# Graph convolution edge stage: how many pairs of edge tiles are in flight between four engines

## What is computed

```
h = silu(edge_scalars @ fc_w1 / sqrt(8))       # 8 scalars per edge, 64 hidden
w = h @ fc_w2                                  # 256 weights per edge: w_a, w_b, w_c, w_d
xg = y[edge_src]                               # 256 features gathered per edge
mid = w * xg, times the 4 numbers edge_attr    # products per edge
agg = segment_sum(mid, edge_dst)               # added up by destination node
```

## Time and profile before

| | |
|---|---|
| median of three runs | 5709.57 us |
| the profiled execution, its own time | 5680.69 us |
| its span | 5678.8 us |
| busy over the span: PE, weight loads, DVE, ACT, POOL | 72%, 53%, 54%, 44%, 53% |
| edge stage, from its first `collect` to the last `add` | about 227 to 2001 us |

### The profile page before, as it was taken

How to read it: one execution, slowest core, us unless ns; L and a number is a source line. 1 busy time by engine, 2 the same in 40 slices (tenths; PEclk the granted TensorE clock), 3 DMA queues, 4 the chain that set the end, 5 groups by cost and what they waited for, 6 DMA issues and landing times. The chain is left out here.

```text
span 5678.8 us, 102477 instructions
## 1 busy us (share of the span) xinstructions
PE 4061.7 (72%) x21623; PEld 3009.8 (53%) x21624; DVE 3040.8 (54%) x7561; ACT 2499.3 (44%) x7826; POOL 3007.1 (53%) x3072
## 2 busy tenths in 40 slices
PE   2789998988998885477777777754267777777770
PEld 1577777777777773344455444532144545544450
DVE  5766666666665655345554444542245444454457
ACT  2566666766666622233333333321133333333342
POOL 2255554555555502566666666512456666666645
PEclk7899999999999997666665666665566666566665
DMA  3322222222222223344443344311334333444424
GB/s 116 105 70 70 72 72 67 73 70 70 71 70 69 71 93 100 98 117 114 115 116 105 113 116 116 98 31 44 99 104 114 111 109 114 116 114 116 115 68 138
DMA packets 253117, 533.46 MB, mean 94 GB/s; under 512 B 65502, under 2 KB 139673, under 8 KB 252916
## 3 DMA queue, kind: packets, MB, share of 16 engines
q0 software_dynamic: 136768, 380.16, 24.2%
q1 hardware_dynamic: 109128, 145.00, 8.1%
q10 hardware_dynamic: 7020, 6.40, 0.3%
HBM read 489.95 MB, written 41.38 MB: 94 GB/s over the span
## 5 line engine op out<-in xcount | busy, mean ns | idle before, releaser
L1118 POOL DMA_INDIRECT arena<-h_rows,idx x1856 | 1904.0, 1026 | 1244.6 <-issue 498.6
L1282 PE MATMUL ps<-arena,z 128*128 128x264 f32 x3712 | 1657.4, 597 | 413.4 <-DVE arena L1391 273.0
L1282 PEld LDWEIGHTS ps<-arena,z 128*128 128x128 f32 x3712 | 973.8, 288 | 739.5 <-issue 469.1
L634 POOL DMA_INDIRECT arena<-y_rows,idx x928 | 878.0, 946 | 841.9 <-DVE arena L819 573.9
L709 ACT ACTIVATE arena<-arena 128x128 f32<-128x128 f32 x3712 | 1133.0, 388 | 348.7 <-DVE arena L803 258.4
L1399 DVE TENSOR_TENSOR z<-ps,z 128x264 f32 x928 | 400.7, 432 | 1134.8 <-PE ps L1282 630.1
L765 PEld LDWEIGHTS ps<-arena 128*128 128x128 f32 x5568 | 808.4, 200 | 64.5 <-issue 8.2
L765 PE MATMUL ps<-arena 128*128 128x128 f32 x5568 | 810.4, 283 | 6.5 <-issue 6.3
L1186 ACT ACTIVATE z<-z 128x256 f32<-128x256 f32 x928 | 380.5, 410 | 949.3 <-PE ps L1282 609.8
L762 PE MATMUL ps<-arena 128*128 128x256 f32 x1856 | 630.9, 423 | 183.3 <-ACT arena L709 127.8
L1178 ACT ACTIVATE z<-iota,dst_x 128x128 f32<-128x128 f32 x1856 | 642.9, 394 | 94.9 <-ACT z L1186 4.0
(11 more groups left out here) (231 smaller groups left out, 3079.8 us busy)
## 6 DMA issues: line engine op xcount, KB each, us to landing
z<-lo_rows SPq DMA_DIRECT2D x116, 512.0 KB
arena<-h_rows,idx POOLq DMA_INDIRECT x1856
arena<-y_rows,idx POOLq DMA_INDIRECT x928
z<-seg_rows SPq DMA_DIRECT2D x232, 64.0 KB
h_rows<-arena SPq DMA_DIRECT2D x98, 132.0 KB, 1.7
arena<-h_rows SPq DMA_DIRECT2D x98, 132.0 KB, 2.1
res_rows<-z SPq DMA_DIRECT2D x98, 128.0 KB, 1.7
arena<-res_rows SPq DMA_DIRECT2D x98, 128.0 KB, 2.1
```

Of the source, the lines that this page charges most:

```text
L634: pool.indirect_dma_start(out=s.ring[:, r, 0:width], out_offset=None, in_=table, in_offset=bass.IndirectOffsetOnAxis(ap=s.idx[:, u, n:n + ...
L1118: pool.indirect_dma_start(out=ring[:, u * SCORED + n, :], out_offset=None, in_=h_rows, in_offset=bass.IndirectOffsetOnAxis(ap=s.idx[:, u, ...
L1282: last = t.matmul(ps[:, bank[q % 4], 0:ROW], sel[:, q % SELS, k, :], ring[:, u * SCORED + 2 * q + k, :], start=(k == 0), stop=(k == 1))
```

## The change

Everything between the engines gets more buffers, and each engine works further ahead in its list:

- `msg`, `sel` and `eq` have four buffers (pair mod 4). `eq` and `e8` become buffers of their own outside the arena, and the others are laid out anew in it.
- The ring has 16 slots, one per slot of a group. The gather of slot n of group g waits until the products of the same place in group g-1 are done, for each pair of slots.
- The second layer of a pair writes one bank: the 512 columns of bank 2 + (pair mod 4). For this `w2` is 512 wide, `fc_w2` stands in rows 0 to 63 of its left half and in rows 64 to 127 of its right half, and the rest is zero. Both matmuls take all 128 rows of `h2`.
- `select` is one comparison of 256 columns in place of two of 128, with both operands broadcast.
- Order for pair n: PE does `first(n+4)` (every other time), `second(n+2)`, `collect(n)`; ACT does `weights(n+2)`, then `silu(n+4)`; DVE does `messages(n+1)`, `select(n+3)`, `add(n-1)`.
- New waits: `weights` waits for `agg_ok` of four pairs before, `messages` too, `select` waits for `sel_ok` of four pairs before, and `second` waits for `msg_ok` of four pairs before. Before, the count of `agg_ok` that `select` waited for stood for the first and the third.

The diff, cut to its core:

```diff
-RING = 8
+RING = GROUP
...
-        s.w2 = sb("w2", [P, FEAT])
+        s.w2 = sb("w2", [P, 2 * FEAT])
...
-            if n % 2 == 0 and not (isinstance(g, int) and g == 0 and n < RING):
-                pool_wait(pool, s, msg_ok, g * 8 + n // 2 - RING // 2 + 1)
+            if n % 2 == 0 and not (isinstance(g, int) and g == 0):
+                pool_wait(pool, s, msg_ok, (g - 1) * 8 + n // 2 + 1)
...
-                sp.dma_start(s.w2[h * 64:(h + 1) * 64, 0:FEAT], a["fc_w2"]).then_inc(wt, 16)
+                sp.dma_start(s.w2[h * 64:(h + 1) * 64, h * FEAT:(h + 1) * FEAT], a["fc_w2"]).then_inc(wt, 16)
...
+            def weights(g, u, n):
+                pair = g * IN + n
                 act.wait_ge(eq_ok, pair + 1)
+                if not early(pair, 4):
+                    act.wait_ge(agg_ok, pair - 3)
...
             def group(g, u, final=False):
+                for n in range(IN):
+                    if not (final and n + 2 >= IN):
+                        weights(*ahead(g, u, n + 2))
+                    if n % 2 == 0 and not (final and n + 4 >= IN):
+                        silu(*ahead(g, u, n + 4))
+                    if n == 0 and not final:
+                        stage(g + 1, 1 - u)
...
                 for k in range(2):
-                    rows = slice(64 * k, 64 * k + 64)
-                    last = nc.tensor.matmul(ps[:, 2 + 2 * b + k, 0:FEAT], h2[rows, q % 2, b, :], s.w2[rows, 0:FEAT], start=True, stop=True)
+                    last = nc.tensor.matmul(ps[:, 2 + n % 4, k * FEAT:(k + 1) * FEAT], h2[:, n // 2 % 2, n % 2, :], s.w2[:, k * FEAT:(k + 1) * FEAT],
+                                            start=True, stop=True)
...
             def group(g, u, final=False):
+                for n in range(IN):
+                    if n % 2 == 0 and not (final and n + 4 >= IN):
+                        first(*ahead(g, u, n + 4))
+                    if not (final and n + 2 >= IN):
+                        second(*ahead(g, u, n + 2))
+                    collect(g, u, n)
...
-                if not (isinstance(g, int) and g == 0 and q == 0):
-                    dve.wait_ge(agg_ok, pair - 1)
-                for k in range(2):
-                    last = v.tensor_scalar(eq[:, b, k, :], s.iota[:, :], s.dst_x[:, bass.ds(pair * 2 + k, 1)], None, ALU.is_equal)
-                last.then_inc(eq_ok, 1)
+                if not early(pair, 4):
+                    dve.wait_ge(sel_ok, pair - 3)
+                v.tensor_tensor(eq[:, n % 4, :, :], s.iota[:, :].unsqueeze(1).broadcast_to([P, 2, P]),
+                                s.dst_x[:, bass.ds(pair * 2, 2)].unsqueeze(2).broadcast_to([P, 2, P]), ALU.is_equal).then_inc(eq_ok, 1)
...
             def group(g, u, final=False):
+                for n in range(IN):
+                    if not (final and n + 1 >= IN):
+                        messages(*ahead(g, u, n + 1))
+                    if not (final and n + 3 >= IN):
+                        select(*ahead(g, u, n + 3))
+                    if n:
+                        add(g, u, n - 1)
+                    elif not (isinstance(g, int) and g == 0):
+                        add(g - 1, 1 - u, IN - 1)
```

More of the change, by code:

```diff
@@ L652, in conv_edges, with ahead, early @@
     eq_ok = s.sem("eq_ok")
-    got = s.swdge("ring", RING, [SLOTS // RING * 16] * RING)
+    got = s.swdge("ring", RING, [GROUPS * 16] * RING)
     got8 = s.swdge("got8_", 2, [0, 0])
-    yg = s.ring[:, :, 0:FEAT]
-    e8, h2 = s.e8, s.h2
+    e8, h2, eq, msg, sel = s.e8, s.h2, s.eq, s.msg, s.sel
     i8 = s.i8[:, :].unsqueeze(2)
-    msg = s.work[:, 0:2048].rearrange("p (b k f) -> p b k f", b=2, k=2)
-    sel = s.work[:, 2048:4096].rearrange("p (b k c n) -> p b k c n", b=2, k=2, c=4)
-    eq = s.eq
     w8 = s.w8[:, :].rearrange("p (q m) -> p q m", q=8)
     ps = s.ps
+    IN = GROUP // 2
     tail = (GROUPS - 1) % 2
+    def ahead(g, u, n):
+        return (g, u, n) if n < IN else (g + 1, 1 - u, n - IN)
+    def early(pair, n):
+        return isinstance(pair, int) and pair < n
     with nc.Block() as block:
@@ L708, in weights @@
                     for c in range(4):
-                        last = nc.scalar.activation(sel[:, b, k, c, :], eq[:, b, k, :], ACT.Copy, scale=s.edge_x[:, c, slot])
+                        last = nc.scalar.activation(sel[:, n % 4, k, c, :], eq[:, n % 4, k, :], ACT.Copy, scale=s.edge_x[:, c, slot])
                 last.then_inc(sel_ok, 1)
             def group(g, u, final=False):
-                for q in range(4):
-                    if q < 3:
-                        silu(g, q + 1)
-                    elif not final:
-                        silu(g + 1, 0)
-                    for b in range(2):
-                        weights(g, q, b)
-                    if q == 1 and not final:
+                for n in range(IN):
[4 more added lines that the diff above has]
+                    if n == 0 and not final:
                         stage(g + 1, 1 - u)
             stage(0, 0)
-            silu(0, 0)
+            silu(0, 0, 0)
+            silu(0, 0, 2)
+            for n in range(2):
+                weights(0, 0, n)
             run_tiles(act, GROUPS - 1, 2, group)
@@ L729, in _, with first @@
             pe.wait_ge(wt, 16 * (GROUP + 2))
-            def first(g, u, q):
+            def first(g, u, n):
+                q = n // 2
+                k = g * (IN // 2) + q
                 if q == 0:
                     pe.wait_ge(got8[u][0], (g - u) * 8 + 16)
-                if not (isinstance(g, int) and g == 0 and q < 2):
-                    pe.wait_ge(h_ok, g * 4 + q - 1)
+                if not early(k, 2):
+                    pe.wait_ge(h_ok, k - 1)
                 for b in range(2):
-                    last = nc.tensor.matmul(ps[:, q % 2, b * P:(b + 1) * P], w8[:, 2 * q + b, :], e8[:, u, :], start=True, stop=True)
+                    last = nc.tensor.matmul(ps[:, q % 2, b * P:(b + 1) * P], w8[:, n + b, :], e8[:, u, :], start=True, stop=True)
@@ L739, in first, with second @@
                 last.then_inc(pre_ok, 1)
[L741 to L746 removed]
+            def second(g, u, n):
+                pair = g * IN + n
+                pe.wait_ge(h_ok, g * (IN // 2) + n // 2 + 1)
+                if not early(pair, 4):
+                    pe.wait_ge(msg_ok, pair - 3)
@@ L754, in collect @@
                 pe.wait_ge(msg_ok, pair + 1)
                 pe.wait_ge(sel_ok, pair + 1)
-                if not (isinstance(g, int) and g == 0 and q == 0):
+                if not early(pair, 2):
                     pe.wait_ge(z_ok, pair - 1)
-                o = ps[:, 6 + b, :]
+                o = ps[:, 6 + n % 2, :]
                 for k in range(2):
-                    m = msg[:, b, k, :]
+                    m = msg[:, n % 4, k, :]
                     o4, m4 = (x[:, 256:512].rearrange("p (q f) -> p q f", q=4) for x in (o, m))
-                    nc.tensor.matmul(o[:, 0:256], sel[:, b, k, 0, :], m[:, 0:256], start=(k == 0), stop=False, skip_group_check=True)
+                    nc.tensor.matmul(o[:, 0:256], sel[:, n % 4, k, 0, :], m[:, 0:256], start=(k == 0), stop=False, skip_group_check=True)
@@ L763, in collect @@
                     for c in range(3):
-                        last = nc.tensor.matmul(o4[:, c:4:3 - c, :], sel[:, b, k, 1 + c, :], m4[:, 0:c + 2:c + 1, :],
+                        last = nc.tensor.matmul(o4[:, c:4:3 - c, :], sel[:, n % 4, k, 1 + c, :], m4[:, 0:c + 2:c + 1, :],
                                                 start=False, stop=(k == 1 and c == 2), skip_group_check=True)
@@ L769, in group @@
             def group(g, u, final=False):
[L770 to L784 removed]
+                for n in range(IN):
[4 more added lines that the diff above has]
+                    collect(g, u, n)
             first(0, 0, 0)
+            first(0, 0, 2)
+            second(0, 0, 0)
+            second(0, 0, 1)
             run_tiles(pe, GROUPS - 1, 2, group)
             group(GROUPS - 1, tail, True)
[L788 removed]
         @block.vector
```

119 lines of the change are left out of this document (47 added, 72 removed).

## The result

After the change the kernel takes 5813.8 us (median of four runs, 5810.8 to 5826.8), before it 5712.6 (four runs, 5692.4 to 5727.1): ratio 1.0193, with an interval of 1.0162 to 1.0223. It is **101 us slower**, not 158 faster. The profiled execution took 5826.8 us, 13 above its median.

A forecast was written before the change was run, and what follows sets the result against it. PE was taken to bound the edge stage. Of 264 us lost there, 92 stay and a slower pace costs 14, so 158 us are won: median 5709.6 to 5552 us, range 5460 to 5690.

The forecast's parts named there:

- Second layer: PE's second layer on all 128 rows: 0.03 us more per pair, +14 us, pace 3.285 us; at most +107 us.
- The price of 204 us: PE's second layer: by the skill alone, undoing half-height packing costs 0.44 us per pair, +204 us; not the value taken.
- The waits: PE's halts in the edge stage: slack grows from 0.8 to 3.15 us; of 264 us lost, 92 stay and 172 go.
- DVE: DVE's single comparison of 256 columns takes 0.43 us against 0.48 for two; 1.0 us to spare, nothing on the path.
- ACT: ACT's copies and silu take 2.9 us, every other pair without silu: costs nothing, 0.4 us to spare, the next bound.
- POOL and the ring: POOL's gathers, 2.66 us a pair, issued up to eight pairs ahead in place of four: priced at nothing.
- Fill and drain: Start and end of the stage: DVE's zeroing comes first in its list before and after, so nothing changes.
- the idle time before L770: Sign of success: PE's idle time before the first matmul of `collect` falls from 183 us to under 70.
- the clock: Sign of success: PE's granted clock in the stage rises from 0.95 to 0.98 or more.
- the sign of being wrong: One stated sign of failure: PE's idle time in the changed kernel is as long as before.
- The slower rival: Gathers bunch on POOL and hold back PE's counts: 4.05 us a pair, 105 us more, 5815 us; chance 0.10.
- Its condition: A count of PE is held back whenever POOL issues, and arrives 1.32 us after its last gather.

The follow-up runs named there:

- experiments 3 and 6: Kernel before with only the full-height second layer: 5816.7 us, ratio 1.002; kernel before without its row gathers: 5486.8 us, ratio 0.937.
- experiment 9: Kernel before with only the ring of 16 slots in place of 8, freed slot by slot: 6337.9 us, ratio 1.095.
- experiment 7: Changed kernel with POOL's gathers at most eight rows (four pairs) ahead of the products: 5823.4 us, ratio 1.0049 to before.
- experiments 4 to 6: Changed kernel without row gathers: 5517.7 us; with plain transfers by SP in their place: 5516.9 us; kernel before without row gathers: 5486.8 us.
- experiment 11: Kernel before with gathers tied one by one to alternate DVE steps: 5825.3 us, ratio 1.0063; changed kernel again, same chip: 5917.9 us, ratio 1.0232.
- experiment 2: Changed kernel itself, run again on a chip where before takes 5829.6 us: 5916.3 us, ratio 1.0206.
- experiment 12: Changed kernel, earlier index copy, a POOL fill awaited behind each row gather; with gathers tied to DVE steps 5583.3 us, without 5533.3 us.

## Why the prediction was wrong

By its own steps:

1. *Second layer*: right. Four records take 0.87 us with `collect` behind them (1008.62 to 1009.49), PE's pace is 3.289 us a pair against a forecast of 3.285, and the edit alone is all of it (experiments 3 and 6: 15.7 us for 14). The price of 204 us, which the prediction derived from the Trainium skill ("TensorE: Matmul & The Clock Gate", Part 3, Packing small matmuls), did not come. The trace of before agrees with the page that the half-height records start together (658.394 and 658.401 us). But going from full to half height and back costs 0.10 us each time, which takes back nearly all that this wins.
2. *The waits*: this is the step that failed. It took the delay of a count, 4.6 us, as a given, and set a slack of 3.15 us against it. 92 us were to stay, and 370 did: the pairs of the stage less 3.289 us each, from first to last `collect`. As far as the delays of before go, the slack was large enough: above 3.15 us they had 35 us in all, not even the 62 allowed for them (the one read as 4.6 is 4.7 by its rows, and the longest is 5.3). But these aren't the delays that the changed kernel met; there it was 254 us. The delay grows with POOL's run of gathers. A count may come within the run (34 of the 79 late ones do, 6.5 us or more after its start) or up to some 2.7 us after its end (experiment 9). And the run grows with the slack: experiment 7 has the slack with before's lead of the gathers, its runs are 5.0 long in place of 2.8, and it wins nothing. That engines which work further ahead free more slots at once is the reading that fits this.
3. *DVE*: right. The comparison takes 0.416 us (0.43 forecast), and DVE is no bound.
4. *ACT*: right as to the bound (its busy time is 1184 us of 1902), but the index copy that it makes once per group became the wait behind which POOL has ten gathers to make up.
5. *POOL and the ring*: the second step that failed. "POOL issues up to eight pairs ahead in place of four" was priced at nothing, since the waits for landed rows were small. The price is what a longer lead lets POOL do to PE. Holding the lead at four pairs takes back 93 us where the change had lost 87, the earlier index copy about 60.
6. *Fill and drain*: about right. The last matmul of the first `collect` starts at 235.1 us, before at 230.9.

Of what would show it, the idle time before L770 came out nearly as told, 76 us for "under 70". That was half a test, and the clock spoke against it (0.93 where 0.98 or more was expected): the lost time had moved to L773 and into the clock, and only the sum of all of PE's idle time, 196 us before (183.3 + 2.0 in the earlier trace rows, 6.5 before L765, 4.2 before L738) and 240 now, shows it. That is the sign of being wrong which the prediction named, an idle time as long as before.

The slower rival gave 4.05 us a pair and 5815 us; measured are 4.09 and 5814. Its condition, that a count is held back whenever POOL issues, is right in part: without the gathers no count is late (experiments 4 to 6), but some come through within a run, and on two chips all do. Its rhythm is not right: it has two pairs at a time in steps of 8.1 us, where the trace shows single halts of DVE, of 2.6 to 7.7 us, in or behind runs of gathers, with undisturbed pairs between them, and PE itself held up, of which it knew nothing. So the agreement of the numbers is partly luck. It had 0.10, by one stretch without waits that spoke against it. That stretch ends where the rows do, in a halt of the same kind, on DVE and on PE:

```profile
664.41 0.48 DVE L803 TENSOR_SCALAR arena<-iota,dst_x 128x128 f32<-128x128 f32 x2 [3.17 <-remote]
...
667.58 1.19 PE L762 MATMUL ps<-arena 128*128 128x256 f32 x2 [1.98 <-ACT arena L709]
```

This, and the five gathers of the earlier trace rows beside the late count of the earlier trace rows, deserved more than "whether POOL is the cause these rows don't tell".

## What to carry to other kernels

When a count comes late, find out what its delay depends on before a deeper pipeline is set against it: a delay that grows with how far the engines run ahead can eat the slack it is given. Where one engine issues gathers in runs, a longer ring is a change to the length of those runs, and its price stands in other engines' rows; look for idle time "on issue" in the middle of a sequence that waits for nothing. Measure on more than one chip, with the kernel before beside it each time.

## What the runs showed of the hardware

- While POOL issues a run of indirect gathers, on three of the five chips and on that of the first result, semaphore counts of PE reach DVE and ACT late, by up to 10.8 us at runs of up to 11 (experiment 11), 13.6 at runs of 13 (experiment 9) and 21.4 at the 24 gathers with which the changed kernel's stage begins, and after 8 to 9 us of the run (1017.7 to 1025.9 in experiment 9) PE itself starts only a record or two every 0.7 to 2.8 us. With the same bytes in plain transfers issued by SP neither is seen (no count of sums over 0.15 us late, clock 1.00).
- On two other chips it isn't there: before takes 5021 and 5022 us in place of 5713 to 5830. In the traces there no count of sums is over 0.15 us late, run or not. Why the chips differ is open. The edge stage is not all of the difference: what follows it, with 1856 gathers by POOL, takes 3282 us there and 3748 on the chip of experiment 2 (both with the edit of experiment 7); those gathers weren't varied.
- A short fill on POOL between two gathers puts them 2.0 us apart in place of 1.25, though it takes 0.22 us itself (experiment 12, where POOL also waits for the fill's end).
